# Idle-time TensorE products, two-bank state inputs and an earlier weighting in the delta-rule stage of a four-layer kernel

## The reference

```python
def delta_rule_chunkwise(q, k, v, beta, chunk=32):
    A = jnp.einsum('bhncd,bhned->bhnce', kbc, kc)
    T = jnp.linalg.inv(eye + jnp.tril(A, -1))
    u = T @ vc
    w = T @ kbc
    def body(S, inp):
        q_i, k_i, u_i, w_i = inp
        attn = jnp.where(tri, jnp.einsum('bhcd,bhed->bhce', q_i, k_i), 0.0)
        u_i = u_i - w_i @ S
        o_i = q_i @ S + attn @ u_i
        S = S + jnp.einsum('bhcd,bhce->bhde', k_i, u_i)
        return (S, o_i)
local_mix = p[..., 0:1] * v + p[..., 1:2] * local_short + p[..., 2:3] * local_long
o = w_global[..., None] * delta_out + (1.0 - w_global)[..., None] * local_mix
o = o * rsqrt(mean(o * o, -1) + EPS) * rms_w
return o.reshape(Bx, Lx, H * DV) @ Wo
```

## Time and profile before

| | us |
|---|---|
| median of 3 runs (lowest, highest) | 609.99 (609.53, 613.34) |
| the profiled execution's own time | 612.65 |
| its span in the profile | 610.9 |
| TensorE busy, share of the span | 545.2 (89%) |
| VectorE | 406.9 (67%) |
| ScalarE | 324.7 (53%) |
| GpSimd | 175.1 (29%) |
| mean granted clock of TensorE | 0.932 |

### The profile page before, as it was taken

How to read it: one execution, slowest core, us unless ns; L and a number is a source line. 1 busy time by engine, 2 the same in 40 slices (tenths; PEclk the granted TensorE clock), 3 DMA queues, 4 the chain that set the end, 5 groups by cost and what they waited for, 6 DMA issues and landing times.

```text
span 610.9 us, 17361 instructions
## 1 busy us (share of the span) xinstructions
PE 545.2 (89%) x7412; PEld 377.7 (62%) x7412; DVE 406.9 (67%) x773; ACT 324.7 (53%) x574; POOL 175.1 (29%) x333
## 2 busy tenths in 40 slices
PE   4699999999999999999999996996998659888993
PEld 2345555555555557877777774774676658666672
DVE  5697989999999825263634437447798572576774
ACT  2327888887888875656555544656605300134441
POOL 7000111445445421010101024238980370010101
PEclk9999999999999999999999998997999665559998
DMA  4778657374250000010000000032734100000011
GB/s 116 149 216 208 191 142 162 68 162 67 62 100 4 5 2 1 0 28 10 0 2 1 1 0 1 2 70 38 139 75 85 23 3 4 5 1 0 2 34 34
DMA packets 54050, 33.80 MB, mean 55 GB/s; under 512 B 38853, under 2 KB 45509, under 8 KB 53974
## 3 DMA queue, kind: packets, MB, share of 16 engines
q1 hardware_dynamic: 48822, 31.65, 23.0%
q10 hardware_dynamic: 5152, 1.05, 1.1%
HBM read 20.83 MB, written 9.44 MB: 50 GB/s over the span
## 4 chain that ended last, share of the span: by engine, by line
PE 71%; DVE 10%; DMA 7%; ACT 7%; issue 3%; SPq 1%; POOL 1%; POOLq 0%; ACTq 0%; DVEq 0%
PE ps L1761 9%; PE ps L1746 8%; PE ps L1513 7%; PE ps L1515 6%; PE ps L1514 6%; PE ps L1861 6%; DMA qst<-shift_sb 5%; PE ps L1725 3%; PE ps L1927 2%; PE ps L2056 2%; PE ps L2057 2%; PE ps L1893 2%; ACT prob L682 2%; PE ps L1994 2%; PE ps L1603 1%
## 5 line engine op out<-in xcount | busy, mean ns | idle before, releaser
L1204 DVE TENSOR_REDUCE nmx<-ps 128x1 f32<-128x1024 f32 x128 | 154.1, 1217 | 19.4 <-PE ps L1726 17.9
L682 ACT ACTIVATE prob<-ps 128x512 f32<-128x512 f32 x256 | 137.5, 597 | 27.0 <-PE ps L1746 26.8
L1761 PE MATMUL ps<-prob,vp 128*32 128x128 f32 x2048 | 78.9, 278 | 0.0
L1746 PE MATMUL ps<-qst,kst 50*128 50x512 f32 x256 | 73.6, 492 | 4.9 <-ACT prob L682 3.4
L1761 PEld LDWEIGHTS ps<-prob,vp 128*32 128x32 f32 x2048 | 49.1, 109 | 39.8 <-ACT prob L682 22.6
L1077 DVE TENSOR_TENSOR h_lo<-hf,h_hi 128x512 fp32r<-128x512 f32 x48 | 33.1, 689 | 52.5 <-ACT h_hi L591 50.2
L1513 PE MATMUL ps<-h_hi,w_lo 128*128 128x512 f32 x144 | 58.2, 404 | 2.4 <-DVE h_lo L1077 2.4
L1515 PE MATMUL ps<-h_hi,w_hi 128*128 128x512 f32 x144 | 56.9, 395 | 0.0
L1514 PE MATMUL ps<-h_lo,w_hi 128*128 128x512 f32 x144 | 56.8, 394 | 0.0
L1725 PE MATMUL ps<-kst,qst 48*128 48x512 f32 x128 | 53.0, 415 | 3.4 <-DMA kst<-k_scratch 3.3
L1726 PE MATMUL ps<-kst,qst 48*128 48x512 f32 x128 | 51.7, 405 | 0.0
(11 more groups left out here) (248 smaller groups left out, 1107.5 us busy)
## 6 DMA issues: line engine op xcount, KB each, us to landing
qst<-q_scratch SPq DMA_DIRECT2D x31, 192.0 KB, 4.4
kst<-k_scratch SPq DMA_DIRECT2D x31, 192.0 KB, 5.0
w_raw<-L_ffn_h_w SPq DMA_DIRECT2D x8, 256.0 KB, 3.4
kd<-ka SPq DMA_DIRECT2D x8, 256.0 KB, 6.2
X<-L_attn_x SPq DMA_DIRECT2D x4, 256.0 KB, 5.3
qst<-shift_sb SPq DMA_DIRECT2D x64, 4.0 KB
q_scratch<-w_hi SPq DMA_DIRECT2D x2, 512.0 KB, 5.5
k_scratch<-w_lo SPq DMA_DIRECT2D x2, 512.0 KB, 3.1
```

The source lines that it names most:

```text
L682: nc.scalar.activation(prob[:, n % PROBS, GT * (t % 2):GT * (t % 2) + GT], ps[:, RINGB + i % RING, :], ACT.Exp, scale=SCORE_SCALE).then_in ...
L1204: nc.vector.tensor_reduce(nmx[:, u % 2, j:j + 1], pair, AX.X, ALU.max, negate=True).then_inc(max_done, 1)
L1746: nc.tensor.matmul(ps[:, RINGB + i % RING, :], kst[r:r + 50, p, P * t:P * t + P], half_of(qst[r:r + 50, p, :], u % 2), start=True, stop=Tr ...
L1761: last = nc.tensor.matmul(ps[32 * j:32 * j + 32, PVB, P * half:P * half + P], vp[:, h, t, :], prob[:, n % PROBS, c:c + P], start=(t == 0), ...
```

## The change

There are four parts.

1. `inputs_of_state` writes two banks per batch instead of four (512 columns in each), and `copy_b` reads them from there. The number and size of the instructions stay.
2. A helper `keep_busy(bank, n)` issues n products of 128x128 by 128x512 into a bank whose content nobody reads. The four ahead of the inverse stay. New are 5 and 8 around the first `inputs_of_state`, 5 and 2 around the second, one in each scan step 1 to 27, and 3, 4 and 6 behind the scan: 60 in all.
3. On VectorE the weighting of the last two groups and the sign matrix `sw0` move ahead of the second `place_u` and `transitions`. On GpSimd the additions of the first two groups move ahead of the memset of the state.
4. `project` of the first group is issued one step earlier, and VectorE's `transposed(0)` ahead of `add_y4(1)` and `stats3(1)`.

```diff
                 for c in range(4):
-                    pair_banks = ps[:, B_BANK[b] + 2 * (c // 2):B_BANK[b] + 2 * (c // 2) + 2, 0:256]
-                    last = nc.scalar.copy(bc[:, b, c].rearrange("p (k n) e -> p k n e", k=2),
-                                          pair_banks.rearrange("p k (n d e) -> p k n d e", d=2, e=C)[:, :, :, c % 2, :])
+                    last = nc.scalar.copy(bc[:, b, c], ps[:, B_BANK[b] + c // 2, :].rearrange("p (n d e) -> p n d e", d=2, e=C)[:, :, c % 2, :])
...
-            pool.wait_ge(uw_psum, B)
-            nc.gpsimd.memset(state[:, 0], 0.0).then_inc(state_zeroed, 1)
-            pool.wait_ge(g_ready, 2)
             for i, g in enumerate(FINAL):
+                if i == 2:
+                    pool.wait_ge(uw_psum, B)
+                    nc.gpsimd.memset(state[:, 0], 0.0).then_inc(state_zeroed, 1)
+                    pool.wait_ge(g_ready, 2)
...
             weigh(0)
             weigh(1)
+            weigh(2)
+            weigh(3)
+            dve.wait_ge(signs_in, 16 * 6)
+            nc.vector.tensor_tensor(sw0[:], k0[:, 0, :], k0[:, 1, :], ALU.subtract)
             place_u(nc.vector.tensor_copy, dve, 1, (2, 3))
             transitions(1)
-            dve.wait_ge(signs_in, 16 * 6)
-            nc.vector.tensor_tensor(sw0[:], k0[:, 0, :], k0[:, 1, :], ALU.subtract)
-            weigh(2)
-            weigh(3)
...
             norm3(0)
+            transposed(0)
             add_y4(1)
             stats3(1)
-            transposed(0)
...
+            def keep_busy(bank, n):
+                for _ in range(n):
+                    nc.tensor.matmul(ps[:, bank, :], sw1[:, 0, 0:P], sw1[:, 1, :], start=True, stop=True)
...
             transition_products(0)
+            keep_busy(7, 5)
             inputs_of_state(0)
+            keep_busy(7, 8)
...
             transition_products(1)
+            keep_busy(3, 5)
             inputs_of_state(1)
+            keep_busy(3, 2)
...
+                if j < 28:
+                    keep_busy(3, 1)
...
+                if j == 28:
+                    project(0, (0, 1))
                 if j == 29:
-                    project(0, (0, 1))
-                if j == 30:
                     project(0, (2, 3))
...
             o_to_features(1, (0, 1, 2, 3))
+            keep_busy(0, 3)
...
             project(1, (0, 1, 2, 3))
+            keep_busy(0, 4)
             x3_transposes(0)
+            keep_busy(0, 6)
```

More of the change, by code:

```diff
@@ L1902, in inputs_of_state @@
                         for h in range(4):
-                            last = nc.tensor.matmul(ps[32 * h:32 * h + 32, B_BANK[b] + 2 * p + n // 4, 2 * C * (n % 4):2 * C * (n % 4) + 2 * C],
+                            last = nc.tensor.matmul(ps[32 * h:32 * h + 32, B_BANK[b] + p, 2 * C * n:2 * C * n + 2 * C],
                                                     ka[r, 8 * b + n, h, 0, :], u_blocks[r, n, h].rearrange("p d e -> p (d e)"), start=True, stop=True)
@@ L1931, in _ @@
             pe.wait_ge(fir_tok_ready, 4)
+            def keep_busy(bank, n):
+                for _ in range(n):
+                    nc.tensor.matmul(ps[:, bank, :], sw1[:, 0, 0:P], sw1[:, 1, :], start=True, stop=True)
             pe.wait_ge(signs_ready, 1)
-            for _ in range(4):
-                nc.tensor.matmul(ps[:, 7, :], sw1[:, 0, 0:P], sw1[:, 1, :], start=True, stop=True)
+            keep_busy(7, 4)
             filtered_to_tokens(0)
```

## The result

| | before | changed |
|---|---|---|
| median of 4 executions, us (lowest, highest) | 610.30 (609.53, 613.34) | 602.66 (599.01, 619.8) |
| profiled execution's own time | 612.65 | 602.81 |
| mean granted clock in it | 0.932 | 0.986 |

The ratio to before is 0.984, with a 95% interval of 0.981 to 0.988. The forecast was 595.7 with a range of 592 to 603.5: faster by over 1%, as said, and 7 us short of what was said. Of the 16 executions of the changed kernel in this document five took 619.77 us or more, with a mean clock of 0.942 or less, against three of the 81 of the kernel before over 616 us, and the ratios leave both out, which is kind to the change.

What follows compares the result with a forecast made beforehand. It took TensorE's 5.45 us wait for VectorE's late first state and the half clock through the scan as the bound; 5.8 + 5.8 + 2.7 = 14.3 us off 612.65 gave 598.35, carried to the median 595.7, range 592 to 603.5.

Steps and rivals of the forecast that it cites:

- A: From the first inverse product to the first scan product: scan begins at 493.2 instead of 498.96, gaining 5.8 us (4.5 to 7.0).
- plus 0.6: Before the second placing: time added for `sw0` on VectorE, after 6.3 us for four weighting instructions.
- The clock: Around and in the scan: added 128x512 products keep PEclk at 1.00 from 470 to the end, instead of 0.50.
- rival 1: Clock falls in `begin_outputs` and returns within the scan; 4.7 us lost against the forecast, 600.4 us; chance 38%.
- B: The scan, first step's product to last add, 34.0 us before: full clock gains 5.8 us (8 to a loss of 4.4).
- 0.26 + 0.37 + 0.23 for the added product = 0.86: Scan steps 4 to 19 at full clock: `begin_outputs` records, the rest, added product; 0.86 instead of 1.10 us, gaining 3.9.
- Steps 1 to 3: First scan steps, up to the add at 504.40: 3.5 us instead of 4.94, three added products included; 1.4 gained.
- Rival 2: The scan is bound by issue, not clock: steps 1 to 19 get 0.23 us longer each, about 605.4; chance 6%.
- Steps 20 to 30: Last scan steps, 10.9 us before: only transposes and projections on the path get faster; 0.5 us gained.
- C: Behind the scan, last add to next blend: 12.5 us instead of 15.24, gaining 2.7 us (1 to 4).

Runs made afterwards that it cites:

- order alone: The changed kernel without the 60 added products, keeping the VectorE and GpSimd moves, two-bank inputs and earlier projection; 607.58 us, ratio 0.995 to before.
- second profile: The changed kernel itself run once more, unaltered, beside the kernels with other product groupings; median 606.77 us, ratio 0.993, profiled execution 607.06.
- products alone: The changed kernel with all its products, but weighting, sign matrix and GpSimd's additions put back where they were before; 626.78 us, ratio 1.027.

## Why the prediction was right or wrong

- **A, up to the scan: right in size, in part by luck.** 5.44 against 5.8. The weighting took 11.63 us for eight against 11.4 forecast, the placing began at 485.95 against 485.9, although everything ahead of it ran 1.29 early. The step "plus 0.6" for `sw0` was low: it took 1.75 in the midst of GpSimd's additions, and that used up the early start. What hid this miss of 1.15 is another: from `transitions(1)` to the scan the prediction kept the 3.15 of before, and it took 2.13, since `begin_outputs` ran without the pauses it had had there. GpSimd's additions beside the weighting took 1.60 to 1.73 each, as the prediction had it from the rows (1.67) and not the 1.95 of a lock held for a whole instruction (the Trainium skill, SBUF — State Buffer, "SBUF: two separate sides"). The prediction saw rightly that VectorE would come after ScalarE, but let the second inverse's clock carry part of the gain; order alone shows that it carried none. And the products ahead of the scan, priced at nothing behind their waits, cost about 1.5 in the second profile, where the wait was gone.
- **The clock: right, but less firm than it looked.** 1.00 throughout in the profile, and the fall in `begin_outputs` of rival 1 did not come in it. The second profile of the same kernel has a fall at 520.9. The prediction had no case for a clock that holds in one execution and not in the next, and that the time fell inside its range is in part luck: 602.66 lies in 592 to 603.5, the 606.77 of the second set does not.
- **B, the scan: right clock, wrong size.** The term that was mis-sized is "0.26 + 0.37 + 0.23 for the added product = 0.86". The 0.63 was 0.68. The 0.23 was 0.41: a price read from products that stood in a row, used for one that stands alone between 32x32 and 64x32 matmuls. An ordinary step became 1.09, and the sixteen, a few longer ones among them, 18.18 us (1.14 in the mean) against the 13.8 forecast (16 x 0.86): 4.4 of the 5.2 us by which B fell short, 3.7 of it by these two terms and the rest by the longer steps. The prediction named over 1.1 apart at full clock as a sign of being wrong; with 1.09, and 1.14 in the mean, the adds stood right at that mark. Steps 1 to 3 gained 0.77 instead of 1.4, most of it for the same cause, three products; the 4.94 that the prediction set them against is a slip as well, since its own rows give 504.40 - 498.96 = 5.44.
- **Rival 2** gave 605.4 by a scan that the clock doesn't speed up. The small gain in B looks like that and the mechanism is not: without a product a step goes from 0.99 to 0.68 with the clock.
- **Steps 20 to 30: right.** 0.40 against 0.5.
- **C, behind the scan: right in size.** `norm3(0)` ended 4.7 us behind the last add (4.9 forecast). `first` began 7.6 behind it (7.0): the transposes stood 529.97 to 530.98 behind four products without a use. The blend began 12.72 behind it (12.5). As in A, the order had the larger part in it, 2.09 of the 2.52: the order alone gives 13.15, with the clock at 0.50 for the first 6 us and then back by itself.
- **The sum.** 14.3 was forecast and 9.84 came in the profiles, of which 1.29 is not the change's. By the ratios to before (one minus the ratio, times before's median) the change gave 9.6 us at first and 4.5 when it ran again, the order alone 3.1, and the change without its products in the scan 4.8. So the products around the scan bring 1.7 by the ratios and 3.2 by the medians (604.41 against 607.58; eight of the ten executions with them lie below all seven without); whether the 27 in it bring anything lies between -0.3 and 4.8 and stays open.

## What to carry to other kernels

Price an added instruction at the place where it stands: between matmuls of other tile sizes a product cost 0.41 us here, behind one of its own kind 0.23, and that difference in 19 steps (3.4 us) is more than half of what the full clock was to bring in the scan (5.8). Remove the wait by order first, which here gave 3.65 of the 5.44 us in its stage with nothing added: products for the clock with a wait of 3 us left behind them made the kernel 2.7% slower. A product put into a wait is free only while the wait is there: five of them cost about 1.5 us in the profile where the inverse came late. Look at several executions before trusting that a clock is held, since one profile shows only one history of it.

## What the runs showed of the hardware

- With TensorE busy for 5.00 of 5.00 us on 32x32 and 64x32 records, and one 128x512 product per 1.71 us among them, the clock stayed at 1.2 GHz to the end of the scan (products alone). One such product per 1.09 us held 2.4 GHz through the scan in one profile of the change, and the level was lost at 520.9 in another. A product in each step held the level in one profile and did not bring it back in another. What the chip goes by is not shown by these runs.
- With one product in every other step the level was lost 16 us into the scan, with one of 256 columns in every step 10 us into it, each in one profile.
- A lone 128x512 product between matmuls of other tile sizes cost 0.41 us at 2.4 GHz and 0.72 at 1.2, one of 256 columns 0.30 and 0.51: 0.18 to 0.19 and 0.29 to 0.30 of it did not go by the columns, and a second product right behind the first did not pay it again (0.23 to 0.24).
- `sw0`, a subtraction of two uint8 operands, took 0.68 us on VectorE before, where it started 0.15 ahead of GpSimd's addition, and 1.75 to 1.77 in the midst of such additions, more than the float operations there (6.76 for four, 1.69 each).
- The placing of batch 1 started at 485.95 with a second inverse of 3.95 us and at 486.01 with one of over 5.4: a faster TensorE moved nothing where VectorE came last. In the second profile of the change, with the inverse late and slow (5.50) and five products behind it, TensorE came last, and the scan began 1.6 later behind the start of A.
